# Thirteen wide products without use in every iteration of a recurrent stage's TensorE program

## The reference, cut to what matters

```python
def step(S, inp):
    q_t, k_t, v_t, b_t = inp
    v_new = (v_t - jnp.einsum('bhd,bhdm->bhm', k_t, S)) * b_t[..., None]
    S = S + jnp.einsum('bhd,bhm->bhdm', k_t, v_new)
    o_t = jnp.einsum('bhd,bhdm->bhm', q_t, S)
    return (S, o_t)
```

## Time and profile before

| what | value |
|---|---|
| median of three runs | 3272.19 us |
| the profiled execution's own time | 3270.95 us |
| span in its trace, first to last instruction | 3269.1 us |
| TensorE busy with matmuls | 2601.0 us (80%) |
| VectorE busy | 2126.1 us (65%) |
| ScalarE busy | 1595.1 us (49%) |
| mean granted TensorE clock | 0.862 |

### The profile page before, as it was taken

The page is one execution under the profiler, slowest core; times in us unless marked ns, Lnnn a source line. Parts: engine busy times, 40 slices in busy tenths (PEclk is TensorE's granted clock), DMA queues, the critical chain, the costliest instruction groups (busy, mean ns, idle before and its releaser), DMA issues. The chain is left out here.

```text
span 3269.1 us, 110359 instructions
## 1 busy us (share of the span) xinstructions
PE 2601.0 (80%) x45968; PEld 1940.2 (59%) x45968; DVE 2126.1 (65%) x5160; ACT 1595.1 (49%) x2896; POOL 1107.2 (34%) x1092
## 2 busy tenths in 40 slices
PE   4578888888888887886787888888987898897666
PEld 2355555556555555654566666667776666675443
DVE  4878998888899888886352111122323577677996
ACT  5455555555555554551143333344444666656442
POOL 0000343333333332334235555555554333233000
PEclk8778898888888888886698989989999899999877
DMA  2000122222112221222256777677779676673521
GB/s 68 8 10 4 63 75 70 70 70 68 61 64 77 70 72 61 70 103 79 70 182 214 223 224 225 218 228 231 238 223 359 219 272 220 235 259 139 221 100 26
DMA packets 191587, 448.68 MB, mean 137 GB/s; under 512 B 34034, under 2 KB 83700, under 8 KB 182772
## 3 DMA queue, kind: packets, MB, share of 16 engines
q1 hardware_dynamic: 129652, 284.26, 27.6%
q0 software_dynamic: 52224, 148.97, 12.0%
q10 hardware_dynamic: 9216, 8.39, 0.8%
HBM read 266.07 MB, written 175.42 MB: 135 GB/s over the span
## 5 line engine op out<-in xcount | busy, mean ns | idle before, releaser
L1041 POOL DMA_INDIRECT scr_xs<-xn_r,idx x512 | 534.5, 1044 | 1183.5 <-PE ps L473 458.3
L1067 POOL DMA_INDIRECT scr_ys<-y,idx_t x576 | 572.5, 994 | 733.9 <-issue 496.4
L712 PE MATMUL ps<-xT,wr 128*128 128x256 f32 (+1 forms) x2560 | 600.0, 380 | 123.1 <-issue 117.2
L2060 DVE TENSOR_TENSOR h<-sg,ps 128x256 f32<-128x256 f32 x320 | 125.2, 393 | 714.8 <-ACT sg L1337 434.7
L712 PEld LDWEIGHTS ps<-xT,wr 128*128 128x128 f32 x2560 | 458.8, 201 | 192.3 <-issue 142.5
L720 PE MATMUL ps<-wr,h 128*128 128x256 f32 x1152 | 324.8, 402 | 63.2 <-ACT y L1345 61.7
L1345 ACT ACTIVATE y<-ps,of_row 128x256 f32<-128x256 f32 x576 | 245.8, 476 | 179.9 <-remote 78.3
L1337 ACT ACTIVATE sg<-ps 128x256 f32<-128x256 f32 x320 | 117.0, 366 | 383.0 <-remote 186.8
L720 PEld LDWEIGHTS ps<-wr,h 128*128 128x128 f32 x1152 | 226.9, 203 | 102.7 <-issue 71.7
L527 PE MATMUL ps<-sq,w_proj 128*128 128x512 f32 x512 | 259.1, 644 | 5.0 <-issue 2.3
L1685 DVE TENSOR_TENSOR tu<-tu,tmp 128x60 f32<-128x60 f32 (+14 forms) x480 | 242.5, 505 | 16.5
(11 more groups left out here) (268 smaller groups left out, 4256.0 us busy)
## 6 DMA issues: line engine op xcount, KB each, us to landing
wr<-in_wexp SPq DMA_DIRECT2D x224, 384.0 KB
xt<-scr_xs SPq DMA_DIRECT2D x256, 280.0 KB
yg<-scr_ys SPq DMA_DIRECT2D x64, 1024.0 KB
scr_ys<-y,idx_t POOLq DMA_INDIRECT x576
scr_xs<-zeros SPq DMA_DIRECT2D x64, 140.0 KB
xt<-scr_xs SPq DMA_DIRECT2D x64, 140.0 KB
x_in<-in_x SPq DMA_DIRECT2D x64, 128.0 KB
x_res<-in_x SPq DMA_DIRECT2D x64, 128.0 KB, 2.7
```

Source lines behind the costliest of these rows:

```text
L712: last = pe.matmul(ps[:, bank, half * TILE:half * TILE + wide], wr[:, w % NW, at:at + EI], xT2[:, t % NH, k, 0:wide], start=k == 0, stop=k ...
L1041: nc.gpsimd.indirect_dma_start(xs[int(i >= FIRST)][:, :], bass.IndirectOffsetOnAxis(idx[:, i % NR, c, k:k + 1], 0), xn_r[:, i % NR, c, :], ...
L1067: nc.gpsimd.indirect_dma_start(ys[int(t >= NTH[0])][:, :], bass.IndirectOffsetOnAxis(idx_t[:, t % NRT, r:r + 1], 0), y2[:, t % NY, r, :], ...
```

## The change

Two helpers are added to TensorE's program. Each runs n products of 128x128 weights (the identity) with 256 columns of `w_proj`. The result of one goes to the half of bank RU from which `right_side` has already read, of the other it is added to a half of bank QP that nothing reads. No semaphore and no wait is added; a waiting instruction has them in front of it or behind it. In one iteration with all steps there are thirteen: one in the middle of each of the four `solved` and the four `to_output`, three in front of the waits of `from_state(j, 0)` (not for j = 0), and two in front of the waits of `to_output(j, 3)`.

```diff
+            def busy_ahead(n):
+                for _ in range(n):
+                    pe.matmul(ps[:, RU, 0:D], identity[:], w_proj[:, 0, 0, :], start=True, stop=True)
+
+            def busy_behind(n):
+                for _ in range(n):
+                    pe.matmul(ps[:, QP, D:2 * D], identity[:], w_proj[:, 0, 0, :], start=False, stop=True,
+                              skip_group_check=True)
...
@@ solved(j, c), in the loop over u, behind the four quadrants' products
+                    if u == H // 2:
+                        busy_ahead(1)
...
@@ the loop over j
                 if C:
+                    if j:
+                        busy_ahead(3)
                     from_state(j, 0)
...
                 if Ps:
                     ranks(p)
                 if C:
+                    busy_behind(2)
                     to_output(j, 3)
                     to_state(j, 3)
```

## The result

The changed kernel took 3316.22 us (median of four runs, 3309.72 to 3321.99) where the kernel before, timed beside it, took 3272.90 us. The ratio is 1.0131, with a 95% interval of 1.0107 to 1.0155. Forecast were 3256 us and a range up to 3300; the change is slower, and the time lies outside the range. Timed again on another chip it was 1.0137 (1.0114 to 1.0161), 3286 against 3247 us.

The account below looks back on a forecast made before the run. VectorE was taken as the nearer bound, but TensorE's speed at the turn. The terms sum to -1.1 us an iteration, -16 us over fourteen turns, 0 for the last two: 3256 us; 8-in-10 range 3226 to 3300.

Parts of the forecast that it names:

- (a): `pairs(b_, 0)` at the turn: 2.2 us saved by the high clock, less 0.6 for new pauses; gain 1.6 us.
- (e): Two products behind `ranks`, one each in `solved(j, 3)` and `to_output(j, 3)`: 1.9 us, mostly hidden; mean cost 0.4 us.
- The clock: At the turn, wide products would lift TensorE's clock from 0.50 and 0.57 to over 0.8.
- fourth rival: The clock at the turn stays low, so the added products cost more: 3333 us; chance 0.10.
- third rival: Instruction supply holds the quadrant blocks, higher clock only lengthens pauses: +1.0 us an iteration, 3292 us; chance 0.16.
- (b): `shared_down` at the turn runs faster at the high clock; gain 0.3 to 1.1 us, taken as 0.4.
- (c): The product in `solved(j, 0)`, between `pairs(b_, 0)` and `pairs(b_, 1)`: cost 0.47 us, bounds 0 and 0.9.
- (d): Three products in front of `from_state(j, 0)`: 1.4 us at the high clock, hidden in TensorE's waits; cost 0.
- (f): Five products in `to_output` of chunks 0, 1, 2 and `solved` of chunks 1, 2: 2.4 us, hidden by VectorE's solve; cost 0.
- The last two iterations: Added products nearly all on the path, 12 us, against faster wide products: taken as 0, bounds -8 and +12.

Follow-up runs that it names:

- e4: The kernel before plus one wide product in the middle of `pairs(b_, 0)` in each iteration, 14 in all; 1.0037.
- e13: The changed kernel with only five products kept, three in front of `from_state(j, 0)` and two behind `ranks`; against the kernel before 1.0004.
- e8_before: The kernel before, unchanged, run for a trace on the chip of the experiments; 0.9993.
- e1: The same kernel as e13, on the chip where the kernel before took 3054 us; against the kernel before 1.0005.
- e7: The kernel before plus three single products, in the middle of `solved(j, 0)`, `solved(j, 3)` and `to_output(j, 3)`; 1.0071.
- e10: The three single products of e7 moved from mid-block to behind their block's last product and semaphore; against the kernel before 1.0041.
- e14: The kernel before plus five single products, in `to_output` of chunks 0, 1, 2 and `solved` of chunks 1, 2; 1.0047.
- e12: The changed kernel with the thirteen products left out of the last two iterations; against the kernel before 1.0095.
- e3: The same kernel as e14, on the chip where the kernel before took 3054 us; against the kernel before 0.9991.

## Why the prediction was wrong, point by point

Two steps made the difference. The gain of (a) was to come from the clock, and a pause took it. And (e) set four products against a wait that can hide two of them. A turn was to be 1.1 us shorter and is 1.6 us longer.

**The clock: right.** At the turn it rose from 0.50 to 1.00. The fourth rival falls. The engine was busy there for 9.24 of 12 us and is busy for 9.29 of 12 us, so what changed is not its idle time but the wide products in it.

**(a) `pairs(b_, 0)`: wrong in its main term.** 1.6 us were to be gained and 0.1 to 0.4 came (4.23 to 4.09, 4.32 to 3.96). The low clock did set the block before, as e4 shows. But a second limit lies right under it. Without the pause the 128 records took 3.8 us in the mean and now take 2.6, and the pause without a wait grew from 0.41 to 1.45 us, past the 1.3 us that the third rival named as the point from which it decides. I had allowed 0.6 us for this, "a pause of that size in half of the cases"; eleven turns of twelve had one of 1.27 us or more. e13 shows it without the cost of the singles: its five products take the low clock's share of the block from 96% (e8_before) to 36%, the block goes from 4.32 to 4.05 us, and the time stays (1.0004). That the pause is the supply of instructions is what the packets of q8 say, by their times and by the place of the pause in the stream; a run that changes the supply alone was not made.

**(b) `shared_down`: nothing gained.** It went from 4.25 to 4.36 us where 0.4 less was forecast.

**(c) The product in `solved(j, 0)`: mis-sized**, 0.71 to 0.88 us for 0.47. The price came from sixteen wide records behind each other. A lone one between quadrant products costs 0.63 us at the high clock and 1.15 at the low one. What the rest of the growth is, no run shows.

**(d) The three in front of `from_state(j, 0)`: right.** They move it by 1.1 us, and it gives back 0.6 to 0.9 by the clock; e1 and e13 say nothing lost, nothing gained. One reading was wrong: at 969 us the row puts the end of the 1.96 us to ScalarE's copy of the output rows (L1156), which follows `to_output(j, 3)`, and not to the new state.

**(e) The four before the new state: the step that made the slowdown.** 0.4 us were forecast, since all four were set against the 1.97 us of waiting for u_sb and 0.78 us of slack. But only the two behind `ranks` stand in that wait. The one in `solved(j, 3)` stands in front of the result from which u_sb is made, and the one in `to_output(j, 3)` behind u_sb. The two behind `ranks` are hidden (2.18 to 2.02 us from the end of `solved(j, 3)` to `to_output`, with both in it). But `solved(j, 3)` grew by 1.1 to 1.2 us and `to_output(j, 3)` by 0.5 to 0.7. The slack that I counted, 0.78 us between `to_state` and L1707 at 969 us, is used up: VectorE now waits for `to_state`, 20.4 us more in thirteen iterations, 1.6 us in each, and the singles of e7 make most of that without the others. Behind the semaphores (e10) the thirteen iterations are no longer than before. The gain of 1 us in `to_output` had been read from one turn that took 3.0 us, with 0.65 us of pauses in it; the mean of twelve was 1.97 us, so there was less to gain.

**(f) The five in the middle: right there, wrong at the ends.** Thirteen iterations hide them (e14). **The last two iterations** were put at 0 with a bound of 12 us; they took 14 us more, and e12 gives back 8 us of it. The wide products that were to get faster there did not pay for them: the clock went from 0.65 and 0.63 to 0.68 and 0.69 only.

What happened is the third rival in kind, at 0.16, but larger: +1.6 us a turn where it had +1.0, and 14 us at the end where it had 6. Its 3292 us are 24 short of the 3316 measured.

## What to carry to other kernels

Before buying clock with filler, look for the limit under the clock: in a block of tiny products a pause without a wait that grows as the work shrinks takes the gain. Count the block's instructions and look at when the instruction queue's packets start and land; here 256 instructions took about 4 us at either clock. Price a filler by a lone instruction of its kind between the neighbours that it will have. Ask of each filler which wait it stands in: here it was hidden between the semaphore that ends one block and the wait that starts the next, and not in the middle of a block for whose end another engine waits (1.0071 in e7, 1.0041 in e10). Better than filler is real wide work that is due anyway: four products of `shared_down` in the wait for the new state gave the high clock in `pairs(b_, 0)` at all twelve turns and 0.4% of time.

## What was not expected of the hardware

Between chips the kernel before differed by 6 to 7% (3054 against 3245 to 3273 us), so times of different chips can't be compared, and ratios only with care: e3 and e14 are one kernel and differ, 0.9991 and 1.0047, beyond their intervals. TensorE's longer pauses without a wait end 1.1 to 1.7 us behind the landing of a packet of 16,384 bytes of instructions, and two such packets started 3.2 us apart at the least. And twelve turns show the quadrant block as nearly indifferent to TensorE's clock: 4.23 us with 91% of it at 1.2 GHz, 4.09 us with 21%.
